# A graph network's edge loop: the last head's weighting moves from VectorE to ScalarE

## The reference

```python
Q = (enh @ Wq + bq).reshape(N, H, D); K = ...; V = ...
mod_k = K[src] + 0.2 * rel[:, None, :]
scores = jnp.einsum('ehd,ehd->eh', Q[dst], mod_k) / D ** 0.5
seg_max = jax.ops.segment_max(scores, dst, num_segments=N)
ex = jnp.exp(scores - seg_max[dst])
denom = jax.ops.segment_sum(ex, dst, num_segments=N)
w = ex / denom[dst]
agg = jax.ops.segment_sum(w[:, :, None] * V[src], dst, num_segments=N)
```

## Time and profile before

| | us |
|---|---|
| median of 3 runs | 1784.93 (1782.49 to 1786.08) |
| profiled execution | 1783.17 |
| its span | 1781.4 |
| second layer's edge loop with weighting at work | 1064 to 1692 of the span |

### The profile page before, as it was taken

The page is one execution under the profiler, slowest core; times in us unless marked ns, Lnnn a source line. Parts: engine busy times, 40 slices in busy tenths (PEclk is TensorE's granted clock), DMA queues, the critical chain, the costliest instruction groups (busy, mean ns, idle before and its releaser), DMA issues. The chain is left out here.

```text
span 1781.4 us, 44262 instructions
## 1 busy us (share of the span) xinstructions
PE 1552.5 (87%) x11207; PEld 1433.5 (80%) x11207; DVE 1586.7 (89%) x3436; ACT 1243.2 (70%) x2988; POOL 1069.4 (60%) x1081
## 2 busy tenths in 40 slices
PE   6979999999999999999718689998999899898843
PEld 3779999999999999999617567777787777787633
DVE  5569999999999999999987579999999999999777
ACT  1568888888888888888545457777776767676614
POOL 0056666666666666666663177777777777777164
PEclk9989999999999999999868899999999999999877
DMA  4466666666666666666303497777777787877523
GB/s 129 161 190 186 185 186 184 188 185 185 181 189 187 185 185 187 184 187 185 104 28 149 171 290 228 231 228 224 228 229 233 217 231 223 230 223 228 193 60 102
DMA packets 165705, 333.98 MB, mean 187 GB/s; under 512 B 31015, under 2 KB 101384, under 8 KB 165092
## 3 DMA queue, kind: packets, MB, share of 16 engines
q0 software_dynamic: 70400, 231.64, 44.6%
q1 hardware_dynamic: 95204, 101.16, 17.8%
HBM read 307.63 MB, written 25.06 MB: 187 GB/s over the span
## 5 line engine op out<-in xcount | busy, mean ns | idle before, releaser
L458 POOL DMA_INDIRECT gath<-edge_in_tab,idx x440 | 464.1, 1055 | 300.6 <-DVE gate_in L882 229.1
L1147 PE MATMUL bank<-weighted,hot 128*128 128x260 f32 x880 | 237.4, 394 | 34.1 <-ACT hot L704 32.7
L1147 PE MATMUL bank<-w_lo,relu_hi 128*128 128x256 f32 x880 | 249.4, 283 | 0.0
L1147 PE MATMUL bank<-w_hi,relu_lo 128*128 128x256 f32 x880 | 249.3, 283 | 0.0
L1147 PE MATMUL bank<-w_hi,relu_hi 128*128 128x256 f32 x880 | 249.2, 283 | 0.0
L609 ACT ACTIVATE relu_hi<-bank 128x512 fp32r<-128x512 f32 x220 | 131.7, 598 | 141.5 <-PE bank L1147 141.5
L471 POOL DMA_INDIRECT kept_more<-kv_tab,idx x176 | 189.8, 1078 | 62.5 <-issue 40.2
L1147 PEld LDWEIGHTS bank<-weighted,hot 128*128 128x128 f32 x880 | 152.5, 192 | 56.3 <-ACT hot L704 41.2
L1150 PE MATMUL bank<-ident,gath 128*128 128x128 f32 x880 | 168.7, 273 | 23.7 <-DVE ea_parts L869 13.3
L891 DVE TENSOR_TENSOR msg<-bank,gate 128x512 f32<-128x512 f32 x220 | 152.2, 692 | 33.6 <-PE bank L1147 17.4
L471 POOL DMA_INDIRECT xs<-kv_tab,idx x132 | 141.6, 1073 | 52.4 <-issue 24.9
(11 more groups left out here) (269 smaller groups left out, 5054.4 us busy)
## 6 DMA issues: line engine op xcount, KB each, us to landing
ea_in<-in_ea SPq DMA_DIRECT2D x440, 64.0 KB
block_row<-row_tab SPq DMA_DIRECT2D x440, 64.0 KB
gath<-edge_in_tab,idx POOLq DMA_INDIRECT x440
kv_tab<-qkv_row SPq DMA_DIRECT2D x26, 258.0 KB, 2.4
edge_in_tab<-node_row SPq DMA_DIRECT2D x26, 256.0 KB, 2.0
xs<-in_x SPq DMA_DIRECT2D x1, 3328.0 KB, 15.0
rows_tab<-xs SPq DMA_DIRECT2D x1, 3328.0 KB, 9.3
rows_tab<-hs SPq DMA_DIRECT2D x1, 3328.0 KB, 10.9
```

The lines of the kernel that those rows point to most:

```text
L458: g.indirect_dma_start(gath[:, q, i, :], None, edge_in_tab, bass.IndirectOffsetOnAxis(ap=idx[:, half, q, i:i + 1], axis=0)).then_inc(gath_ ...
L1147: return nc.tensor.matmul(out_, lhsT=lhs, rhs=rhs, start=start, stop=stop)
```

## The change

In the weighting of a block's values VectorE multiplies three heads (128x390 for both halves) instead of four (128x520). The last head is multiplied on ScalarE by a new stage, `weight_last_head`, of two instructions of 128x65, one a half, each with the weight as a per-partition scale. The stage stands between the one-hot and the distances, with lag 17. It has a semaphore of its own, `last_weighted`. TensorE's sums, GpSimd's gathers and SyncE's load of the output weights wait for it besides `weighted_done`.

```diff
             sp.wait_ge(weighted_done, BLOCKS)
+            sp.wait_ge(last_weighted, BLOCKS)
...
                 after(pool, weighted_done, b - KEEP + 1)
+                after(pool, last_weighted, b - KEEP + 1)
...
+            def weight_last_head(k, q):
+                b = KEEP * k + q
+                half, turn = q // BATCH, q % BATCH
+                act.wait_ge(weights_done, 2 * k + half + 1)
+                after(act, agg_ready, b - 1)
+                at = HEADS * turn + HEADS - 1
+                for i in range(2):
+                    last = s.activation(weighted[:, q % 2, i, VALW - HEADW:], kept(q, HID + VALW - HEADW, HEADW)[:, i, :], ACT.Copy,
+                                        scale=weight_col[:, half, i, at:at + 1])
+                last.then_inc(last_weighted, 1)
...
-            pipeline(act, [(fetch_query, 0), (copy_keys, 1), (copy_weights, 6), (exponents, 5), (one_hot1, 17), (node_distances, 16), (copy_scores, 2)],
+            pipeline(act, [(fetch_query, 0), (copy_keys, 1), (copy_weights, 6), (exponents, 5), (one_hot1, 17), (weight_last_head, 17), (node_distances, 16), (copy_scores, 2)],
...
-                v.tensor_tensor(weighted[:, q % 2, :, :].rearrange("p i (h d) -> p i h d", h=HEADS),
-                                kept(q, HID, VALW).rearrange("p i (h d) -> p i h d", h=HEADS),
-                                weight_col[:, half, :, HEADS * turn:HEADS * (turn + 1)].unsqueeze(3).to_broadcast([P, 2, HEADS, HEADW]),
-                                ALU.mult).then_inc(weighted_done, 1)
+                values = kept(q, HID, VALW).rearrange("p i (h d) -> p i h d", h=HEADS)
+                some = weight_col[:, half, :, HEADS * turn:HEADS * (turn + 1) - 1]
+                v.tensor_tensor(weighted[:, q % 2, :, :].rearrange("p i (h d) -> p i h d", h=HEADS)[:, :, 0:HEADS - 1, :], values[:, :, 0:HEADS - 1, :],
+                                some.unsqueeze(3).to_broadcast([P, 2, HEADS - 1, HEADW]), ALU.mult).then_inc(weighted_done, 1)
...
                 pe.wait_ge(weighted_done, b + 1)
+                pe.wait_ge(last_weighted, b + 1)
```

More of the change, by code:

```diff
@@ L268, in build @@
         idx_seen, rel_in, rel_done, agg_zero = sem("idx_seen"), sem("rel_in"), sem("rel_done"), sem("agg_zero")
-        segments_known, dist1_done = sem("segments_known"), sem("dist1_done")
+        segments_known, dist1_done, last_weighted = sem("segments_known"), sem("dist1_done"), sem("last_weighted")
         def after(engine, signal, n):
```

## The result

The changed kernel took 1818.26 us in the median (1815.29 to 1821.12), the kernel before, measured beside it, 1784.94: a ratio of 1.0186 with an interval of 1.0168 to 1.0205. The forecast was 1798.9, its range ended at 1812. The profiled execution took 1821.12 us around a span of 1819.4, 38 us more than the span before; it is the slowest of the four executions.

What follows compares the result with a forecast made beforehand. VectorE was taken as the batch's clock, except just after the segment maxima, where everybody waits for ScalarE. Regular intervals 8.6, long ones 0.8, first and last 0.8, tail 3.8: +14.0 us, median 1798.9 us; range 1782 to 1812.

Steps and rivals of the forecast that it cites:

- The prices: Edge loop, each block: ScalarE's pair costs 0.48 us, VectorE saves 0.137 us, ScalarE's step grows from 1.98 to 2.46 us.
- Late key copies: After the segment maxima, which end VectorE's step 5: longer ScalarE steps delay a key copy, so VectorE's product starts 0.98 us later.
- the key copy of step 12: ScalarE, seventh step after the segment maxima: this copy ends at 1311.72 us and holds up VectorE's next product.
- VectorE's product of step 13: VectorE, eighth step after the segment maxima: starts at 1311.77 instead of 1310.79 us, +0.98, waiting for ScalarE's key copy.
- the hot of step 6: ScalarE's one-hot in the step after the segment maxima: comes 0.48 us later, at 1296.86 us.
- TensorE's sums ... now wait for the new semaphore also: +0.48 us.: Right after the segment maxima: sums wait for ScalarE's pair, 0.48 us later, delaying the work queued behind them on TensorE.
- All later gathers of the batch slide by about 0.6 us. In a regular batch that is hidden: GpSimd after the segment maxima: late release costs nothing in regular batches; in four long ones +0.62 - 0.41 = +0.2 us.
- the sum: Regular interval between segment maxima: +0.98 us from the late key copy less 0.41 saved by VectorE, +0.57 us.
- VectorE's saving: From the delayed product to the next segment maxima: three shortened instructions give 0.41 us back; other savings fall into waits.
- The tail: After the last segment maxima: ScalarE becomes the clock at 1.61 us a step and SyncE waits for it, +3.8 us.
- A: Rival: VectorE is the bound and ScalarE has room; pair under 0.40 us, 1768 us; chance 0.12.
- C: Rival: key copy later still, the pair costing 0.59 us; 14.6 us more in intervals, 1815 us; chance 0.12.

Runs made afterwards that it cites:

- act_only: Kernel before plus ScalarE's two instructions on a constant tile, written to an unread tile; nobody waits, VectorE weights four heads: 1804.51 us, ratio 1.0102.
- act_gate_b: Kernel before plus ScalarE's pair on a constant tile, output unread, with TensorE's sums waiting for it; repeat on another chip: 1817.48 us, ratio 1.0161.
- no_release: Changed kernel, but ScalarE's pair reads a constant tile and the gathers do not wait for it: 1814.02 us, ratio 1.0155.
- turn7_const: Changed kernel, pair only in the block weighted in the maxima's step, reading a constant tile; sums wait, gathers do not: 1809.91 us, ratio 1.0144.
- turn7_release: Kernel before plus one pair a batch in the maxima's step, output unread; gathers wait for it, TensorE does not: 1823.71 us, ratio 1.0223.
- turn7_b: Changed kernel with the last head on ScalarE only in the block weighted in the maxima's step; repeat on another chip: 1812.99 us, ratio 1.0138.
- dve_only: Kernel before, VectorE weighting three heads, the fourth filled once ahead of the loop and weighted by nobody: 1770.17 us, ratio 0.9902.
- turns0to6: Changed kernel, last head on ScalarE in seven of ten blocks: ratio 1.0164 on a slow chip; repeated as turns0to6_b, 1778.87 us, ratio 0.9950.
- before_weights: Changed kernel with the new stage moved right behind the key copy on ScalarE: ratio 1.0077 on a slow chip; repeated elsewhere, 1784.98 us, ratio 0.9993.
- turns0123: Changed kernel, last head on ScalarE only in four blocks, third to sixth step after the maxima: ratio 1.0169 on a slow chip; repeated, 1783.51 us, 0.9982.

## Why the prediction was wrong, point by point

- *The prices.* Right. The pair costs 0.48 us of ScalarE's time, VectorE saves 0.135 us, ScalarE's step is 2.46 us.
- *Late key copies.* Right in kind, wrong in place, and the near agreement of numbers is luck. The forecast let the key copy of step 12 hold up VectorE's product of step 13. In the trace of the changed kernel (medians of 19 intervals) VectorE's products of steps 7 to 10 start 0.03 us after their copy has ended, so VectorE goes at ScalarE's pace there; that of step 13 starts 0.32 us after it, without a wait. What VectorE has lost by step 10 (1.22 us in the interval of 1369.24) it doesn't make up. In the interval of 1369.24 it also begins the instruction behind each of these four products 0.82 to 1.17 us after the product's start, against 0.60 to 0.77 in that of the earlier trace rows; why is open. act_only gave +0.92 us an interval against a forecast of +0.98, but the forecast held TensorE's wait too: in act_only the hot of step 6 comes only 0.06 us later, not 0.48, and the forecast's own way of adding then gives 0.56. Length and wait together, act_gate_b, are +1.61, or +1.36 at full clock.
- *"TensorE's sums ... now wait for the new semaphore also: +0.48 us."* Mis-sized: +0.68. The old hot had released the sums 0.05 us after its end; the pair's end (1371.05) and the sums' start (1371.29) lie 0.24 apart. The wait alone took act_only from 1804.5 to 1817.5 us. And in the runs where TensorE waits longest there, more of the 19 inner intervals are below the full clock: 8 in no_release, 9 in turn7_const, none in the kernel before. In the changed kernel's own trace it is hardly part of the loss: 18 of 19 intervals are at full clock.
- *"All later gathers of the batch slide by about 0.6 us. In a regular batch that is hidden."* This is the step that failed: a term put at nothing. The slide is 1.5 us (2.75 against 1.24 us behind the maxima), since GpSimd starts 0.94 us after what released it, where I had let it start at once. And it isn't hidden: at the same clock it is 0.68 us in each inner interval (no_release 30.10, the changed kernel 30.78), which over 19 intervals makes some 13 of the 19 us by which the forecast missed. I asked only when the blocks of the next few steps are wanted. Five blocks on, TensorE's keys stand in front of the row ends, which the running maxima wait for: 7.0 us in 9 waits in the changed kernel, 1.4 in 2 before. There was hardly any cover there: in the interval of the earlier trace rows TensorE had waited 0.49 us for a landing in front of these very keys (at 1314.52), and its row ends started at 1315.73, 0.8 us ahead of VectorE's running maxima (1316.52). turn7_release shows what late gathers are worth by themselves, 38 us, there by way of the key copies.
- *What the rest adds up to.* Without the gathers the sum was near, by errors that nearly cancel: length and wait +1.36 for +0.98, VectorE's saving -0.65 for -0.41, together +0.71 for +0.57 (all at full clock). One interval of 34.85 us adds 4 us, the last one 2.6 us where 0.4 were forecast.
- *The costs don't add up.* In turn7_b, where the length is gone, either wait is enough for the whole loss. I had summed lateness along one chain, where, as I now read it, several chains close the same batch with little between them.
- *VectorE's saving.* The forecast gave 0.41 us a batch back. By the times no_release is only 3.5 us under act_gate_b, of 30 us of shorter instructions; at full clock the intervals are 0.65 us shorter.
- *The tail.* Right: +4.0 for +3.8. One-hots stand 1.60 to 1.61 us apart but for one of 1.80, the last starts at 1728.16, and SyncE's loads follow ScalarE's last pair. The chain behind it, answering to the earlier trace rows:
```profile
1728.16 0.51 ACT L706 ACTIVATE hot<-dist,one_col 128x256 f32<-128x256 f32 x1
...
1728.58 0.57 ACT L715 ACTIVATE weighted<-hs,weight_col 128x65 f32<-128x65 f32 x2
...
1730.56 5.39 DMA wo_sb<-in_wo
```
- *The rivals.* A had the right direction for VectorE's saving alone (dve_only, -17 us), and C the right size for a wrong reason: the pair did not cost 0.59 us. A late release of GpSimd should have been a rival of its own: the forecast had it busy for 27.6 of 29.0 us of a batch, which leaves it little slack.

What stays open: the 0.68 us rest on sorted intervals, and no run holds the clock still; why turn7_release costs more than turn7_b, which has both waits; and the one interval of 34.85 us in the changed kernel's trace, in which TensorE waited 2.59 us for a landing and then ran at a mean granted clock of 0.76 for the ten microseconds around it. Why the clock was halved after some waits of 2.28 us and not after others was not explained either.

## What to carry to other kernels

Where work of several engines closes in a loop (here once a batch), its price is set by its place on the loop and not by its length: the same 0.48 us cost 27 us in one block of ten, and in four others nothing that VectorE's saving did not cover. Before adding an instruction between a late event and what it releases, list every semaphore that is raised behind it, and follow each one round to the same event of the next batch, through the DMA queue too. If a stage must go to an engine that stands still for somebody, put it ahead of that wait, not behind it.

## What the runs showed of the hardware

- GpSimd does not start a gather at the moment its wait ends. In the kernel before, VectorE's weighting ended at 1384.54 us and the gather that it released started at 1385.43, 0.89 later; in the changed kernel 0.94 us pass, and in seven such waits of the kernel before 0.88 or 0.89. Gathers that don't wait follow each other in 0.30 us. VectorE's and GpSimd's timelines of the kernel before:
```profile
1383.86 0.68 DVE L1055 TENSOR_TENSOR weighted<-xs,weight_col 128x520 f32<-128x520 f32 x1
```
```profile
1385.43 0.94 POOL L471 DMA_INDIRECT xs<-kv_tab,idx  x1 [1.94 <-DVE weighted L1055]
```
- In turn7_const a stand-still of TensorE of 2.28 us was followed by the lower clock in some batches (sums of 1.65 to 2.07 us) and not in others (1.11 us). So a change that takes away other waits of TensorE can lengthen this one and lose its gain to the clock, as in no_release: most of its waits behind the maxima are 2.27 to 2.29 us, most of the changed kernel's 1.26 to 1.86.
- Chips differ: the kernel before took 1784 to 1787 us on the others and 1985 and 2013 us on two, where engines stood still for longer without a releaser in the profile (GpSimd's gathers of the first layer 158 us in the 800 us from 200 us on in turns0to6, 59 in turns0to6_b). There before_weights lost 0.8%, turns0123 1.7% and turns0to6 1.6%, which on the other chips were level, 0.2% and 0.5% faster. These splits, with more instructions, were worth less on them.
